# Weighing and adding the four experts' outputs with TensorE in the last stage, and the layout that this asks for earlier

## The reference, cut to what matters

```python
h = (x_flat @ W_gat).reshape(M, HEADS, NUM_EXPERTS)
e = leaky_relu(a_src[src] + a_dst[dst], 0.2)          # one per edge and head
agg = softmax_over_edges_of_a_token(e) * h[src], summed over edges, + b_gat
scores = layernorm(agg).reshape(M, HEADS, NUM_EXPERTS).mean(1)
topk_s, topk_i = top_k(scores, 2);  w = softmax(topk_s)
for ei in range(4):
    g = where(topk_i == ei, w, 0).sum(-1)              # the gate, one per token
    hh = gelu(x @ W1[ei] + b1[ei])                     # 128 -> 256
    out = out + g[..., None] * (hh @ W2[ei] + b2[ei])  # 256 -> 128
return x + out
```

## Time and profile before

| what | us |
|---|---|
| median of 3 runs | 8943.4 (8943.16 to 8950.78) |
| the profiled execution | 8939.67 |
| its span | 8937.9 |
| TensorE busy | 3473.0 (39%) |
| VectorE busy | 3842.3 (43%) |
| ScalarE busy | 1988.6 (22%) |
| GpSimd busy | 5388.0 (60%) |

### The profile page before, as it was taken

One profiled execution on the slowest core, in us unless ns is written; L12 is line 12 of the kernel. 1 busy time (PEld: TensorE's weight loads), 2 busy tenths in 40 slices (PEclk: granted clock), 3 DMA queues, 4 the chain that ended last, 5 costly groups with the idle time before them and its releaser, 6 DMA issues. The chain is left out here.

```text
span 8937.9 us, 45998 instructions
## 1 busy us (share of the span) xinstructions
PE 3473.0 (39%) x9579; PEld 1626.4 (18%) x9579; DVE 3842.3 (43%) x7346; ACT 1988.6 (22%) x3855; POOL 5388.0 (60%) x4840
## 2 busy tenths in 40 slices
PE   7888498991012222222222222222223222222134
PEld 4565244440000111011110110111101010100001
DVE  7888798788331212121212121212121212144498
ACT  6777255551011111111111110101010101001011
POOL 4555000001777777777777777777777777777452
PEclk8888699995555656656656656565666565656555
DMA  3343222220111111111111111111111111111166
GB/s 105 120 125 115 70 96 75 82 86 33 18 43 33 42 35 42 35 42 34 42 35 37 39 37 40 37 40 37 40 36 41 36 41 35 41 32 37 44 222 205
DMA packets 344241, 532.42 MB, mean 60 GB/s; under 512 B 159307, under 2 KB 236026, under 8 KB 319098
## 3 DMA queue, kind: packets, MB, share of 16 engines
q1 hardware_dynamic: 196514, 473.73, 15.2%
q0 software_dynamic: 147552, 56.95, 5.5%
HBM read 299.88 MB, written 230.45 MB: 59 GB/s over the span
## 5 line engine op out<-in xcount | busy, mean ns | idle before, releaser
L1136 POOL DMA_INDIRECT e_got<-rows,e_index x4352 | 4629.0, 1064 | 1456.0 <-issue 1456.0
L1594 PE MATMUL ex_y_ps<-ex_hh,w_w 128*128 128x512 f32 x1024 | 934.3, 1067 | 4143.2 <-issue 2577.9
L1629 DVE SCALAR_TENSOR_TENSOR ex_z<-ex_y_ps,w_b,ex_gate 128x512 f32<-128x512 f32 x192 | 144.1, 751 | 3256.4 <-remote 1924.9
L1594 PEld LDWEIGHTS ex_y_ps<-ex_hh,w_w 128*128 128x128 f32 x1024 | 295.9, 318 | 4624.3 <-issue 4115.9
L1612 ACT ACTIVATE ex_hh<-ex_hid_ps,w_b 128x512 f32<-128x512 f32 x512 | 322.5, 684 | 2550.3 <-remote 1756.6
L1126 POOL DMA_INDIRECT e_head<-rows,p_first x1 | 1.2, 1177 | 1194.1 <-issue 1194.1
L1576 PE MATMUL ex_hid_ps<-ex_tn,w_w 128*128 128x512 f32 x1024 | 639.6, 759 | 92.8 <-DMA ex_tn<-norm 67.9
L493 PE MATMUL o_hid_ps<-o_tn,w_w 128*128 128x512 f32 x1024 | 524.2, 594 | 72.0 <-DMA o_tn<-norm 72.0
L1232 DVE TENSOR_TENSOR_SCAN e_out<-e_near,e_out,e_wgt 128x64 f32<-128x64 f32 x1088 | 335.5, 364 | 459.5 <-issue 452.1
L506 PE MATMUL o_y_ps<-o_hh,w_w 128*128 128x512 f32 x1024 | 524.4, 594 | 14.7 <-ACT o_hh L524 14.7
L524 ACT ACTIVATE o_hh<-o_hid_ps,w_b 128x512 f32<-128x512 f32 x512 | 351.0, 687 | 364.8 <-PE o_hid_ps L493 364.8
(11 more groups left out here) (365 smaller groups left out, 6010.3 us busy)
## 6 DMA issues: line engine op xcount, KB each, us to landing
e_got<-rows,e_index POOLq DMA_INDIRECT x4352
kept<-o_kept SPq DMA_DIRECT2D x64, 1024.0 KB, 4.5
ex_gate<-gate SPq DMA_DIRECT2D x64, 1024.0 KB
c_kept<-kept SPq DMA_DIRECT2D x64, 1024.0 KB
sums<-e_out SPq DMA_DIRECT2D x68, 768.0 KB
m_xin<-in_x_dram SPq DMA_DIRECT2D x64, 512.0 KB, 4.6
mid<-m_xm SPq DMA_DIRECT2D x64, 512.0 KB, 2.9
norm<-m_tn SPq DMA_DIRECT2D x64, 512.0 KB, 4.9
```

The lines of the kernel that those rows point to most:

```text
L1136: pool.indirect_dma_start(got[:, at % 2, c, :], None, rows_d, bass.IndirectOffsetOnAxis(ap=index[:, at % 2, c:c+1], axis=0)).then_inc(S["g ...
L1594: last = pe.matmul(self.y_ps[:, :], self.weights.w2[:, e, f, :], self.hh[:, e % 2 * HID + f, :], start=(f == 0), stop=(f == HID - 1))
```

## The change

In the sort stage the second product of each expert swaps its operands: the hidden block is the weight and W2 moves, four products of 128 columns in place of one of 512, so that `kept` holds tokens on the partitions; its bias is left out. In `Ends` the 13 bit steps go into three turns, each of the 5 groups has tables of its own, groups 0 and 1 are built a turn earlier, and VectorE waits for TensorE once, at the end. The finish is written out without loops: one VectorE product per tile multiplies all four experts' outputs by gates that lie in PSUM; TensorE adds the input (a product with the identity), the biases weighted by the gates (4 products of 128 columns) and the 16 blocks (products with the identity, which also turn them back) in PSUM; ScalarE copies the result out. The gates are computed after 12, 20, 28 and 32 turns.

```diff
@@ Outputs.tensor, Outputs.keep
-                pe.matmul(self.y_ps[:, e % 2, :], self.weights.w2[:, e, f, :], self.hh[:, g % 2, :], start=(f == 0), stop=(f == HID - 1)).then_inc(S["y"], 1)
+                for b in range(BLKS):
+                    last_y = pe.matmul(self.y_ps[:, e % 2, b*P:(b+1)*P], self.hh[:, g % 2, b*P:(b+1)*P], self.weights.w2[:, e, f, :],
+                                       start=(f == 0 and b == 0), stop=(f == HID - 1 and b == BLKS - 1))
+                last_y.then_inc(S["y"], 1)
-        act.activation(self.kept[:, r % 2, e, :], self.y_ps[:, e % 2, :], ACT.Identity, bias=self.weights.b2[:, e:e+1]).then_inc(self.S["kept"], 1)
+        act.activation(self.kept[:, r % 2, e, :], self.y_ps[:, e % 2, :], ACT.Copy).then_inc(self.S["kept"], 1)
@@ Ends
-    BITS = (range(0, 4), range(4, 8), range(8, 11), range(11, SHIFT_BITS))
+    BITS = (range(0, 5), range(5, 9), range(9, SHIFT_BITS))
+    def groups(self, k):
+        return range(0, 2) if k == CHUNKS - 1 else range(2, self.BLOCKS // self.GROUP)
...
+        if k >= CHUNKS - 1:
+            if self.x and k == CHUNKS - 1:
+                pe.wait_ge(self.x.S["stt"], EXPERTS * TOKEN_TILES)
+            for g in self.groups(k):
+                pe.wait_ge(S["hot"], g + 1)
+                for m in range(GROUP):
+                    last = pe.matmul(self.pos_ps, self.values[g][:, m*P:(m+1)*P], self.tables[g][:, m, :], start=(g == 0 and m == 0), stop=False)
+            if k == CHUNKS:
+                pe.wait_ge(S["hot"], BLOCKS // GROUP + 1)
+                pe.matmul(self.pos_ps, self.corner[:, :], self.rims[:, :], start=False, stop=True).then_inc(S["hit"], 1)
...
-                if m % GROUP == 0 and g >= 2:
-                    v.wait_ge(S["hit"], g - 1)
@@ Gates.vector
-        if self.split:
-            split = result.rearrange("p b (i j e) -> p b i j e", j=PARTS, e=EXPERTS)
...
+        go(v.tensor_copy(result.rearrange("p (t e b) -> p t e b", e=EXPERTS, b=BLKS), gate[:, :, :].rearrange("p (t b) e -> p t e b", b=BLKS)))
@@ finish_lower
+    GROUPS = (12, 8, 8, 4)
+    CHUNK = P // EXPERTS
+    FIRST = [sum(GROUPS[:i]) for i in range(len(GROUPS) + 1)]
+    TILES = [2 * n for n in FIRST]
+        def tiles_at(k):
+            i = next(i for i in range(len(GROUPS) + 1) if i == len(GROUPS) or k < FIRST[i + 1])
+            if i == 0:
+                return []
+            first, count = TILES[i - 1], TILES[i] - TILES[i - 1]
+            if i == len(GROUPS):
+                return list(range(first, first + count)) if k == TURNS else []
+            n, j = GROUPS[i], k - FIRST[i]
+            return list(range(first + count * j // n, first + count * (j + 1) // n))
 sync:
+                for t in range(TOKEN_TILES):
+                    if t + 4 < TOKEN_TILES:
+                        sp.wait_ge(S["turned"], t + 1)
+                        load(t + 4)
+                    if t:
+                        store(t - 1)
 tensor:
+                for t in range(TOKEN_TILES):
+                    i = group_of(t)
+                    if t == TILES[i]:
+                        pe.wait_ge(S["gated"], i + 1)
+                        need(pe, S["gt"], i)
+                        for n in range(CHUNKS_BEFORE[i + 1] - CHUNKS_BEFORE[i]):
+                            last = pe.transpose(gt_ps[:, n, :], weights.g[:, n*CHUNK:(n+1)*CHUNK, :].rearrange("p b e -> p (b e)"), ident[:, :])
+                        last.then_inc(S["gtp"], 1)
...
+                        pe.wait_ge(S["gt"], i + 1)
+                    u, j = t % 4, t % 2
+                    need(pe, S["fin"], t - 1)
+                    pe.wait_ge(S["ld%d" % u], 32 * (t // 4 + 1))
+                    pe.matmul(out_ps[:, j, :], ident[:, :], xm[:, u, :], start=True, stop=False)
+                    for b in range(BLKS):
+                        col = t * BLKS + b
+                        pe.matmul(out_ps[:, j, b*P:(b+1)*P], brow[:, col % CHUNK, :], gt[:, col // CHUNK, :], start=False, stop=False)
+                    pe.wait_ge(S["mul"], t + 1)
+                    for b in range(BLKS):
                         for e in range(EXPERTS):
+                            last = pe.matmul(out_ps[:, j, b*P:(b+1)*P], kept[:, u, e, b, :], ident[:, :], start=False, stop=(b == BLKS - 1 and e == EXPERTS - 1))
+                    last.then_inc(S["turned"], 1)
 scalar:
+                def evict(upto):
+                    for t in range(done[0], upto):
+                        u = t % 4
+                        act.wait_ge(S["turned"], t + 1)
+                        need(act, S["st%d" % u], 16 * (t // 4))
+                        act.activation(o[:, u, :], out_ps[:, t % 2, :], ACT.Copy).then_inc(S["fin"], 1)
...
+                for n in range(CHUNK):
+                    last = act.activation(brow[:, n, :], rows[:, :], ACT.Copy, scale=mask[:, n:n+1])
...
+                for i in range(len(GROUPS)):
+                    evict(TILES[i] - 3)
+                    weights.scalar(act, i, COLS_OF[i])
+                    evict(TILES[i])
...
 vector:
+                def weigh(t):
+                    u = t % 4
+                    v.wait_ge(S["ld%d" % u], 32 * (t // 4 + 1))
+                    gates = gate_ps[:, t*EXPERTS*BLKS:(t+1)*EXPERTS*BLKS].unsqueeze(2).broadcast_to([P, EXPERTS * BLKS, P])
+                    flat = kept[:, u, :, :, :].rearrange("p e b c -> p (e b) c")
+                    v.tensor_tensor(flat, flat, gates, ALU.mult).then_inc(S["mul"], 1)
...
+                for k in range(TURNS):
+                    if k + 1 < TURNS:
+                        indices(k + 1)
+                    for t in tiles_at(k):
+                        weigh(t)
+                    gathered(k)
+                    if k + 1 in FIRST:
+                        i = FIRST.index(k + 1) - 1
+                        v.wait_ge(S["agg"], k + 1)
...
+                        v.sem_inc(S["gated"], 1)
+                for t in tiles_at(TURNS):
+                    weigh(t)
```

More of the change, by code:

```diff
@@ L1693, in finish_lower @@
-        weighed = sb("weighed", [P, 2, EXPERTS, TOK]); pairs = sb("pairs", [P, 2, TOK]); total = sb("total", [P, TOK])
-        gate_ps = ps("gate_ps", [P, EXPERTS, TOK])
-        def gathered(k): return not isinstance(k, int) or k < TURNS
-        def turns(eng, group, body):
-            first = GROUP * group
-            peeled = (GROUP, 2, 0, 0, 0)[group] if group < 4 else 0
-            for k in range(first, first + peeled):
-                body(k, k % 2, k // 2)
-            if peeled < GROUP:
-                with eng.Fori(0, (GROUP - peeled) // 2) as turn:
-                    for at in range(2):
-                        body(first + peeled + at + turn * 2, at, (first + peeled) // 2 + turn)
@@ L1706, in tiles, with group_of @@
[L1706 to L1709 removed]
+        kept = sb("kept", [P, 4, EXPERTS, BLKS, P]); xm = sb("xm", [P, 4, TOK]); o = sb("o", [P, 4, TOK])
+        gt = sb("gt", [P, HIS // CHUNK, P])
+        out_ps = ps("out_ps", [P, 2, TOK]); gate_ps = ps("gate_ps", [P, HIS * EXPERTS]); gt_ps = ps("gt_ps", [P, 4, P])
+        def group_of(t):
+            return next(i for i in range(len(GROUPS)) if t < TILES[i + 1])
@@ L1724, in last @@
-                def last(k, at, pair):
-                    for t, u, j in tiles(k, at):
-                        need(sp, S["fin"], t + 1)
-                        sp.dma_start(out_d[k - GROUP, :, j*TOK:(j+1)*TOK], o[:, u, :]).then_inc(S["st%d" % u], 16)
-                for group in range(1, GROUPS + 1):
-                    if group < GROUPS:
-                        turns(sp, group, body)
-                    else:
-                        first = GROUP * group
-                        with sp.Fori(0, GROUP // 2 - 1) as turn:
-                            for at in range(2):
-                                body(first + at + turn * 2, at, first // 2 + turn)
-                        for at in range(2):
-                            last(first + GROUP - 2 + at, at, 0)
+                flat = io["b2"].rearrange("e (a c) -> a e c", a=1)
@@ L1738, in _ @@
+                for t in range(4):
+                    load(t)
+                for t in range(TOKEN_TILES):
[4 more added lines that the diff above has]
+                        store(t - 1)
+                store(TOKEN_TILES - 1)
                 for u in range(4):
@@ L1764, in body @@
                         for e in range(EXPERTS):
-                            need(pe, S["mul"], (t - 1) * EXPERTS + e + 1)
-                            pe.matmul(gate_ps[:, e, :], rows.choose[:, e, :], rows.turned[:, j, :], start=True, stop=True).then_inc(S["sel"], 1)
-                for group in range(1, GROUPS + 1):
-                    turns(pe, group, body)
+                            last = pe.matmul(out_ps[:, j, b*P:(b+1)*P], kept[:, u, e, b, :], ident[:, :], start=False, stop=(b == BLKS - 1 and e == EXPERTS - 1))
@@ L1778, in _ @@
-                for group in range(GROUPS + 1):
-                    if group:
```

(9 more changed lines are left out.)

268 lines of the change are left out of this document (88 added, 180 removed).

## The result

The kernel after takes 8976.0 us in the median of eight runs (8965.7 to 8985.6), the kernel before 8945.3 beside it: a ratio of 1.0034, 95% interval 1.0025 to 1.0043. It is **31 us slower**; 42 us faster was forecast. The profiled execution of after has a span of 8980.4 us, that of before 8937.9. Times between chips differ by more than the effects here (the kernel before had medians from 8944 to 8968 us on the chips of this study), so each experiment is told as its ratio to the kernel before on the same chip.

The account below looks back on a forecast made before the run. TensorE's queue was taken to pace the sort and, after the change, the finish. Sort +10, end of attention -20 and finish -32 summed to -42 us: 8902 us forecast, range 8870 to 9050 (8870 to 8925 for the forecast alone).

Parts of the forecast that it names:

- The rival that had the most weight: Sort and finish: weight loads not covered, TensorE's 128-column pitch slower, 5.11 us per ns, 9100 at 150 ns; chance 0.23.
- the low clock: Finish: TensorE stays at 1.2 GHz, 10.2 us a tile, 9184 us in all; chance 0.07.
- Rival 3: Finish: transfers are the bound, 5.85 us a tile for 56 tiles, +30 us, 8932 in all; chance 0.12.
- the finish, -32: Finish: TensorE need not stop for all of VectorE's gates, so the end comes at 8906.2 against 8937.9 us.
- 24 tiles at 5.31: Finish, first group: 24 tiles at TensorE's 5.31 us each, plus 2 us at the low clock, reaching 8648.8 us.
- The stops between groups: Finish: gaps between tile groups of 13.6, 13.6 and 5.8 us, from load, weighing, sums, gates and turning.
- Two fit in PSUM, and the third follows the gates' exponential within the gap: Finish, a group's last three tiles: two await their copies in PSUM, the third is done within the 13.6 us gap.
- the end of attention, -20: End of attention: without the wait and with groups 0 and 1 built earlier, 20 us gained, bounds 10 and 24.
- The wait in the code at that place is the one for `hit`: End of attention: VectorE's 23.2 us idle before the third group of tables was put down to this wait.
- Three groups ... start at about 8270.8: End of attention, turn 68: VectorE's remaining three groups of tables take 14.7 us, starting at about 8270.8.
- It ends at 8285.5, before the last gather lands: End of attention: VectorE's three groups end at 8285.5, so the gather landing at about 8295 is the late one.
- rival 4: End of attention: VectorE's stall comes back, a gain of 10 us for 20, 8912 in all; chance 0.08.

Follow-up runs that it names:

- one_product: After with the sort's second products as before: one of 512 columns in place of four of 128; ratio to the kernel before 1.0022.
- few_loads: After with the finish's 1 MB load of kept done for the first four tiles only; ratio to the kernel before 1.0026.
- half_sums: After with the finish's sums over two of the four experts only, 52 TensorE records a tile instead of 84; ratio to the kernel before 0.9957.
- few_gathers: After with one gather instead of eight in each of turns 12 to 31 of the finish; ratio to the kernel before 0.9976.
- gather_pace: After with GpSimd waiting for TensorE's tiles ahead of each single gather in the finish's turns 12 to 31; ratio to the kernel before 0.9992.
- loop_hook: After with TensorE's finish as loops, gates turned in 16-column chunks, and ScalarE copying two tiles between the gates' square root and exponential; ratio to before 1.0047.
- pace_hook: After with a GpSimd wait ahead of each finish gather and ScalarE copying two tiles between the gates' square root and exponential; ratio to before 0.9979.
- old_ends: After with the places' products as before: two tables, a wait for hit, four bit steps a turn; ratio to the kernel before 1.0048.
- woven: pace_hook with the last three tiles of the first and third groups weighed inside the gates that follow; ratio to before 0.9964, 8910.5 us.
- turn_pace: After with GpSimd waiting for TensorE's tiles ahead of each turn's eight gathers, finish turns 12 to 31; ratio to the kernel before 1.0016.

## Why the prediction was wrong

**Right.** The sort: +10 forecast; +11.4 in the trace, 11 us by one_product, with 111 ns a record as taken. The rival that had the most weight (a pitch over 119.5 ns) fell, and with it the low clock: granted 1.0 in the last tiles. In the finish the way from the positions to the first gather (3 us less forecast, 3.9 seen), from there to the first tile (155.4 us, 155.2 seen), VectorE's product (2.3 us, 2.286 seen) and a tile's pitch (5.31, seen 5.325) all held. By the estimate that I had worked out from the Trainium skill, TensorE: Matmul & The Clock Gate, section Back-to-back issue gap (which names no type beside its 81 ns), with 25 ns more a record, the sort alone would have been 64 us later; the float32 pairs of this case went at 111 ns and don't show it. Rival 3, transfers as the bound, fell with few_loads and half_sums.

**Wrong, the term that decided: the finish, -32.** It came to 616.2 - 571.0 = +45, so 74 us above my 542. Two steps of its chain failed.

1. "24 tiles at 5.31", and the same for the other groups, took the pitch of undisturbed records for stretches in which GpSimd gathers. "A product stream that is never out of work" was said of the clock, and I didn't ask whether another engine could hold it up. few_gathers prices the omission at **53 us**, gather_pace shows that 39.5 us come back when the same gathers are spread. No rival of mine had it. The trace of before holds the same gaps, and I read past them: beside attention's gathers VectorE's scans of one step start 0.70, 1.40 or 2.10 us apart, as in this row of its timeline.

```profile
8229.31 0.38 DVE L1232 TENSOR_TENSOR_SCAN e_out<-e_near,e_out,e_wgt 128x64 f32<-128x64 f32 x1 [1.72 <-issue]
```

2. The stops between groups, 13.6, 13.6 and 5.8 us, measured 22.0, 20.8 and 14.6 in few_gathers: **24 us** more. "Two fit in PSUM, and the third follows the gates' exponential within the gap" is the step: the third tile came behind the exponential, as I wrote, but I had counted the stop from that tile's end as if it were done before. It costs its 5.3 us, and more at 1.2 GHz (8.3 us for tile 23 in few_gathers). And a load for the last tile was weighed 9.0 us after its issue (8629.7 to 8638.7 in few_gathers), where I had 6. loop_hook and pace_hook take 10 and 12 us of the 24 back by the ratios.

few_gathers stands 20.4 us above the forecast's 542.2, less than the 24.4 chiefly because some 4 of the 7 us that I had put in for slow starts lie within the stops; 53.6 and 20.4 are the 74.

**Wrong: the end of attention, -20.** The trace has 10.7 us to the positions, old_ends 12.5 by the ratios and 14.5 up to the finish's first gather. Three steps failed.

1. "The wait in the code at that place is the one for `hit`". The earlier trace rows speaks against it: TensorE's 28 records of groups 0 and 1 start at 8275.9 and end at 8284.9, and VectorE needed the end of the first group alone, which comes some 1 us after it fell idle at 8281.1. It went on only at 8304.3. In old_ends it stands idle for 21.8 us at the same instruction, with `hit` done as well. What held VectorE was not shown. Its idle time ends 13.0 us after the last gather (15.4 in old_ends), and the gaps of TensorE behind attention's last gather, in all twelve kernels with the new class, end 16 to 18 us after it. So the stutter is a candidate for most of the 23 us; no run tests that.
2. "Three groups ... start at about 8270.8". They start at 8293.7; 11.9 us of the difference is what all of attention's end is later by. The two groups that were moved a turn earlier did fit under the wait for gathers: VectorE's attention steps begin at 8225.0, 0.2 us later than before, counted from the last gather. But they take 36.8 us for 20.3, with gaps of 0.7 us and its multiples among them, and so the experts' last tile was added at 8293.1 instead of 8270.1.
3. "It ends at 8285.5, before the last gather lands". Because the groups start late, their idle time counts: 6.4 us in front of one instruction of the fifth group (5.3 to 6.8 us at the same instruction in all twelve kernels), and 3.5 us more in the last chunk, which takes 18.0 us for 14.6. That is rival 4's size, and in part its reason: some 10 of the 23 us of idle time came back in another place.

Together: +11.9 (to the last gather of attention), -10.7 (to the positions), -3.9 (to the finish's first gather) and +45.2 (the finish) make +42.5, which is the difference of the spans (8980.4 - 8937.9).

## What to carry to other kernels

Where GpSimd gathers, price TensorE's stream as two things: the records' pitch, and how many records it may issue before the gathers pause. Here a row of six gathers (7 us, in woven) left no gap and one of 24 cost 18 us, and a wait ahead of each gather, on the progress of the engine beside it, made the kernel 38 us faster without removing any work. Before a wait is put down to a semaphore, look when that semaphore was given: here `hit` was given 22 us before VectorE went on. A gap whose reason is "issue" and whose starts lie a multiple of one number apart is a thing to line up with what the other engines do, in the kernel before too.

When an engine copies tiles out and also takes part in a chain of small steps, count the buffers at the point where it waits inside that chain: the tile that finds no buffer is on the path.

## What was not expected of the hardware

- During an unbroken row of gathers (one each 1.25 us) TensorE of the finish issues some 130 to 167 more records in most rows, then one in 0.70 us or a multiple of it, until 1 to 5 us behind the row. Behind attention's last gather, after turns of 64 gathers each, TensorE's gaps last until 16 to 18 us behind it. The volume of transfers (8 or 299 GB/s) and the fetches of its instructions (81 or 67) make no difference to this; pauses of 2 to 4 us after two to four gathers end it.
- In the same rows TensorE's signal that a tile is done comes late, up to 18.7 us after the tile's last record in after, and never over 0.6 us in few_gathers.
- Pairs of a weight load and a product of 128 columns in float32 ran at 111 ns a pair with gathers beside them and 301 GB/s moving; 790 records of products, of 512 columns among them, filled 100 us (gather_pace).
- Transfers of this stage reached 350 GB/s at a share of 0.94 (half_sums), above the 300 at 0.89 of the earlier trace rows.
- The granted clock was 0.98 over the 100 us of turn_pace's short stutters but fell to 0.5 in the long one (from 8695.7 to 8716.1 us in after, 0.64 on average over 8690 to 8710), so the tile behind it ran at 1.2 GHz.
